# Window attention and convolution on one core: softmax weights as the stationary operand, a new order of the steps

## The reference

```python
x = x + _L0_conv_ref(_gn(x), L0_conv_ac_w, L0_conv_ac_b, L0_conv_qkv_w, L0_conv_proj_w, L0_conv_proj_b)
x = x + _L1_conv_ref(_gn(x), L1_conv_W, L1_conv_bias)
```

```python
g = (x * ac_w[None, :, None, None] + ac_b[None, :, None, None]) * x
g = jnp.clip(g, 0.0, 6.0)
qkv = jnp.einsum('bchw,dc->bdhw', g, qkv_w)
...
attn = jnp.einsum('wnqd,wnkd->wnqk', q, k) * scale
attn = jax.nn.softmax(attn, axis=-1)
o = jnp.einsum('wnqk,wnkd->wnqd', attn, v)
...
out = jnp.einsum('bchw,dc->bdhw', o, proj_w) + proj_b[None, :, None, None]
```

## Time and profile before

| | us |
|---|---|
| median of 3 runs | 1495.81 (1494.65 to 1499.69) |
| the profiled execution | 1495.76 |
| its span | 1494.0 |
| PE busy | 1171.3 (78%) |
| DVE busy | 1232.3 (82%) |
| ACT busy | 994.7 (67%) |
| POOL busy | 620.4 (42%) |

### The profile page before, as it was taken

How to read it: one execution, slowest core, us unless ns; L and a number is a source line. 1 busy time by engine, 2 the same in 40 slices (tenths; PEclk the granted TensorE clock), 3 DMA queues, 4 the chain that set the end, 5 groups by cost and what they waited for, 6 DMA issues and landing times. The chain is left out here.

```text
span 1494.0 us, 56299 instructions
## 1 busy us (share of the span) xinstructions
PE 1171.3 (78%) x21860; PEld 696.7 (47%) x21860; DVE 1232.3 (82%) x1891; ACT 994.7 (67%) x1683; POOL 620.4 (42%) x438
## 2 busy tenths in 40 slices
PE   1288888988898986878747888988898898768875
PEld 1155555655565654333324555555565565423332
DVE  6678778887887985999985878887887888679998
ACT  2768777877787874544425877877787788644442
POOL 7124333433334432565632333333333334336665
PEclk9989999999999997899987999999999999979999
DMA  6143333333333330032324333333333343101111
GB/s 249 55 124 105 114 106 95 123 107 94 114 115 93 124 106 4 29 112 84 112 98 147 111 116 98 109 113 102 104 115 104 104 125 113 30 0 57 42 56 70
DMA packets 115466, 144.93 MB, mean 97 GB/s; under 512 B 21000, under 2 KB 91048, under 8 KB 114216
## 3 DMA queue, kind: packets, MB, share of 16 engines
q1 hardware_dynamic: 115240, 141.44, 29.6%
HBM read 72.16 MB, written 69.24 MB: 95 GB/s over the span
## 5 line engine op out<-in xcount | busy, mean ns | idle before, releaser
L503 ACT ACTIVATE work<-ps,ws 128x512 f32<-128x512 f32 x512 | 337.1, 682 | 61.8 <-PE ps L972 42.8
L734 DVE TENSOR_REDUCE m_all<-ps 128x8 f32<-128x512 f32 x512 | 328.1, 683 | 45.2 <-PE ps L949 44.0
L409 POOL TENSOR_TENSOR work<-work 128x512 f32<-128x512 f32 x128 | 162.7, 1271 | 370.4 <-ACT work L511 370.4
L415 POOL TENSOR_TENSOR g_lo<-work,g_hi 128x512 f16<-128x512 f32 x128 | 145.6, 1158 | 327.9 <-ACT g_hi L548 327.9
L960 PE MATMUL ps<-q_stack,k_stack 128*64 128x64 f16 x8192 | 216.4, 200 | 25.7 <-DMA q_stack<-max_scratch 24.0
L960 PEld LDWEIGHTS ps<-q_stack,k_stack 128*64 128x64 f16 x8192 | 179.4, 114 | 84.3 <-DMA q_stack<-max_scratch 45.4
L972 PE MATMUL ps<-work,v_ext 128*32 128x64 f32 x8192 | 210.1, 226 | 6.5 <-ACT work L503 0.6
L906 PE MATMUL ps<-work,c_hi 128*128 128x512 f16 x384 | 150.5, 392 | 69.6 <-DVE work L825 69.5
L601 ACT CAST work<-work 128x640 f16<-128x640 f32 x128 | 92.0, 720 | 145.6 <-DVE work L821 99.6
L949 PE MATMUL ps<-k_stack,q_stack 128*64 128x256 f16 x2048 | 177.8, 291 | 13.8 <-issue 4.8
L972 PEld LDWEIGHTS ps<-work,v_ext 128*32 128x32 f32 x8192 | 137.2, 110 | 92.0 <-issue 69.3
(11 more groups left out here) (130 smaller groups left out, 2022.9 us busy)
## 6 DMA issues: line engine op xcount, KB each, us to landing
stack_scratch<-work SPq DMA_DIRECT2D x128, 256.0 KB, 2.1
q_stack<-stack_scratch SPq DMA_DIRECT2D x64, 384.0 KB
k_stack<-stack_scratch SPq DMA_DIRECT2D x256, 96.0 KB
stack_scratch<-work SPq DMA_DIRECT2D x128, 128.0 KB, 2.1
out_dram<-work SPq DMA_DIRECT2D x32, 512.0 KB, 2.7
img<-in_x_dram SPq DMA_DIRECT2D x8, 1024.0 KB, 14.2
img<-in_x_dram SPq DMA_DIRECT2D x16, 512.0 KB, 3.9
q_stack<-zero_scratch SPq DMA_DIRECT2D x64, 32.0 KB
```

Source lines behind the costliest of these rows:

```text
L409: g.tensor_tensor(recip[h], sums[h], guess[h], ALU.mult).then_inc(near_done, 1)
L415: g.tensor_tensor(g_lo[:, m, :, e, :], g32.rearrange("p (w q) -> p w q", w=UW), g_hi[:, m, :, e, :], ALU.subtract).then_inc(g_lo_done, 1)
L503: a.activation(probs[:, w % 2, :], ps[:, ST_B + w % 2, :], ACT.Exp, scale=ws[:, R_EXP:R_EXP + 1]).then_inc(exp_done, 1)
L734: v.tensor_reduce(m_all[:, 0, 2 * h:2 * h + 2, p, :], ps[:, S_B + h, :].rearrange("p (g j k) -> p g j k", g=2, k=WIN), AX.X, ALU.max).then ...
```

## The change

- `weigh` swaps the operands: the exponentials (64 columns, f32) are stationary, `v_ext` (now 18 columns: 16 for two heads, 2 for row sums) moves. The result has queries in the rows and, for each of 8 head pairs, 18 columns. Two windows (a pair `p`) are one step of 16 products; there were two steps of 8.
- `divide` takes the exact reciprocal of the sums (128 x 32) and multiplies 256 columns with it. Shuffle, guesses and Newton step are gone.
- `turn` transposes the result back (two f32 transposes for each half of a unit), ACT copies it (`turned`), and `output` is one product with the whole projection matrix.
- `scores_t`, `exps`, `scores` and `row_max` work on two PSUM banks at a time: four steps a unit each, 1024 columns a step on ACT and DVE.
- The first product of scores uses 96 rows, not 128; the zeros that were loaded for it (L307) go.
- v is computed in one step into bank GB, with the two heads of a pair in two halves of the rows. Half of `g_hi` and `g_lo` (a second copy of each) goes.
- The second pass of unit n starts in iteration n at its windows 0 to 3 and ends in iteration n+1 (stage E); the maxima are sent in D; R is two iterations behind.

```diff
-                return {s for s, lead in (("G", 4), ("H", 3), ("B", 2), ("C", 1), ("D", 0), ("R", -1), ("X", -2))
+                return {s for s, lead in (("G", 4), ("H", 3), ("B", 2), ("C", 1), ("D", 0), ("E", -1), ("R", -2))
...
-                        v.stream_shuffle(sums[h], ps[:, PV_B + h, :], [16 + j % 16 for j in range(32)]).then_inc(sums_done, 1)
...
+                        bank = ps[:, PV_B + h, 0:2 * HP * VC].rearrange("p (a c) -> p a c", c=VC)
+                        after(dve, pv_done, d, 2 * h + 2)
+                        v.reciprocal(rec[h], bank[:, :, 2 * HD:VC]).then_inc(rec_done, 1)
...
-                            v.tensor_reduce(m_all[:, 0, 2 * h:2 * h + 2, p, :],
-                                            ps[:, S_B + h, :].rearrange("p (g j k) -> p g j k", g=2, k=WIN), AX.X,
-                                            ALU.max).then_inc(max_done, 1)
+                        v.tensor_reduce(m_all[:, 0, :, p, :],
+                                        ps[:, S_B:S_B + 2, :].rearrange("p h (g j k) -> p (h g) j k", g=2, k=WIN), AX.X,
+                                        ALU.max).then_inc(max_done, 1)
...
+                        a.activation(probs[:, p % 2, :], ps[:, ST_B:ST_B + 2, :].rearrange("p w t -> p (w t)"), ACT.Exp,
...
+                                mm = t_.matmul(ps[64 * w:64 * w + 64, PV_B + p // 2, col:col + VC],
+                                               probs[:, p % 2, at:at + WIN], v_ext[:, md, 2 * p + w, hp, :],
                                                start=True, stop=True)
...
-                            mm = t_.matmul(ps[:, GB, :], pw[:, a, :], o_n[:, :, a, :], start=(a == 0), stop=(a == 1))
+                        t_.matmul(ps[:, GB, :], pw[:, :], o_t, start=True, stop=True).then_inc(proj_done, 1)
...
+                    if "C" in on:
+                        scores(1)
+                    if "E" in on:
+                        weigh(n - 1, me, 2)
                     if "B" in on:
+                        after(pe, v_out, n + 1)
                         after(pe, res_done, n - 2)
                         project(1, GB, k_done)
+                    if "E" in on:
+                        scores_t(n - 1, me, 3)
```

More of the change, by code:

```diff
@@ L308, in one @@
+                        write(d, mb, 1)
                         after(sp, q_sent, d)
+                        after(sp, st_done, d - BUFS)
                         sp.dma_start(q_stack[0:ROWS, mb, :, :],
@@ new lines, in v_rows @@
+                    def v_rows():
+                        r_hi, r_lo = (r[:, 2, :].rearrange("p (h e d) -> p e h d", e=2, d=HD) for r in (w_hi, w_lo))
+                        for w in range(UW):
+                            tok = slice(w * WIN, (w + 1) * WIN)
+                            l_hi, l_lo = g_hi[:, mb, tok], g_lo[:, mb, tok]
+                            for k, (lhs, rhs) in enumerate(((l_hi, r_hi), (l_lo, r_hi), (l_hi, r_lo))):
+                                for e in range(2):
+                                    mm = t_.matmul(ps[64 * e:64 * e + 64, GB, tok], lhs, rhs[:, e, :, :],
+                                                   start=(k == 0), stop=(k == 2))
@@ L977, in output @@
[L977 to L989 removed]
+                                                   q_stack[0:ROWS, mc, 2 * h + gg, tok],
@@ new lines, in scores, with scores_t @@
+                                                   k_stack[0:ROWS, mc, 2 * h + gg, :, tok], start=True, stop=True)
+                        mm.then_inc(s_done, 1)
+                    def scores_t(d, md, p):
+                        after(pe, exp_done, d, p)
+                        for w in range(2):
+                            tok = slice((2 * p + w) * WIN, (2 * p + w + 1) * WIN)
+                            for hp in range(HP):
+                                g, j = hp // 2, 2 * (hp % 2)
+                                for e in range(2):
+                                    mm = t_.matmul(ps[64 * e:64 * e + 64, ST_B + w, hp * WIN:(hp + 1) * WIN],
+                                                   k_stack[:, md, g, j + e, tok], q_stack[:, md, g, tok],
+                                                   start=True, stop=True)
+                        mm.then_inc(st_done, 1)
@@ new lines, in turn @@
+                    def turn(d, h):
+                        after(pe, o_done, d, h + 1)
+                        for a in range(2):
+                            mm = t_.transpose(ps[:, GA, h * 256 + a * P:h * 256 + a * P + P], o_n[h][:, a * P:a * P + P],
+                                              ident[:, :])
+                        mm.then_inc(ot_done, 1)
+                    def output(d):
+                        after(pe, ot_out, d)
+                        t_.matmul(ps[:, GB, :], pw[:, :], o_t, start=True, stop=True).then_inc(proj_done, 1)
```

444 lines of the change are left out of this document (181 added, 263 removed).

## The result

The changed kernel takes 1672.62 us (median, 1664.65 to 1678.25), where the kernel before took 1495.23 us beside it (1493.36 to 1499.69): a ratio of 1.118 [1.113, 1.123]. It is slower, as forecast, but by 177 us, not 59, and the time lies above the range of 1470 to 1615 us. The span of the profiled execution is 1676.5 us, 182.5 more than before.

What follows compares the result with a forecast made beforehand. The keys' loop through DRAM was taken to bound the kernel: 7.7 + 8.3 = 16.0 us a unit instead of 14.74. That gave +29.7 us per image, +59 for two on 1495.76: 1555 us, range 1470 to 1615.

Steps and rivals of the forecast that it cites:

- The second loop: Keys leave DVE, go through DRAM and back to the next unit's scores; 13.9 of 14.74 us, close to the bound.
- The 0.8 us of slack: Room left in the keys' loop of the kernel before: 5.1 + 8.8 = 13.9 of 14.74 us a unit.
- that of the maxima: Maxima written to DRAM and read back: a little later, but used later too, at 9.1 us, so hidden.
- X: Time from a unit's first scores until DVE finishes the keys: 7.7 us, 2.6 more than before.
- L: Time from finished keys through DRAM to their use in the next unit's scores: 8.3 us.
- P: Length of an ordinary attention unit, X + L: 16.0 us instead of 14.74.
- `weigh`'s 1.03: On PE, a `weigh` step of 32 pairs, priced by its f32 loads: 1.03 us, bounds 0.58 and 1.43.
- The clock in ordinary units: PE's clock was taken as low only behind the loop's branch, one unit in three; ordinary units take 16.0 us.
- rival 3: PE's clock falls in ordinary units too, up to +1.6 us each: 1590 to 1600 us if in all; chance 0.18.
- the unit behind the branch: It starts at 1.2 GHz, which makes scores, the first `weigh` and part of a projection longer: 17.6 us.
- The loop's end: PE's pause of 3.6 to 4.0 us at the branch is partly covered by the wait for keys: unit of 17.3 us.
- The tail: Second pass and new stage at an image's end: guesses, POOL products and half an `output` go, transposes and copies come: -3 us.

Runs made afterwards that it cites:

- old_keys: The changed kernel, but the first scores use q and k of the unit before, so no new keys are waited for: 1502.85 us.
- keys_first: The changed kernel with the keys' projection right behind that of q on PE, their copies moved up on ACT and DVE: 1544.15 us, 1.032 of before.
- before_late: The kernel before with only PE's projection of k moved behind the second step of scores: 1654.06 us, 1.107 of before.
- warm: The changed kernel with 30 unread f16 products on PE ahead of the first scores in each full unit: 1624.9 us, 1.088 of before.
- after_vc32: The changed kernel with 32 moving columns in `weigh` in place of 18, the added ones zeros: 1637.14 us, 1.093 of before.
- keysfirst_vc32: `keys_first` with 32 moving columns in `weigh` in place of 18, the added ones zeros: 1501.92 us, 1.004 of before.
- warm2: As `warm`, but without the 30 unread products in the unit right behind the loop's branch: 1615.62 us, 1.084 of before.

## Why the prediction was right and wrong

- **The bound.** Right. The second loop, not DVE, was what the change ran into: taking the wait for keys out (`old_keys`) or most of it (`keys_first`) gives back 180 and 127 us of the 182.5 in the span. The 0.8 us of slack read from the earlier trace rows was the reading that mattered. In the kernel before there was a second such loop beside it, that of the maxima, which the prediction called hidden; in the changed one it is, but `before_late` shows that it was near.
- **X = 7.7, L = 8.3, P = 16.0.** X was 7.7 us in eight of the ten units (of 59) whose part up to the low half of k ran at full clock (7.9 and 8.2 in the others). Right were also `weigh`'s 1.03, the exponential's 1.12 and the order on DVE. L was 7.3 to 8.3 in the eight units at full clock (mean 7.7) and 8.46 over the 59, so that P at full clock was 15.5 on average, not 16.0: L was taken 0.6 us too long for them. The reciprocal of 128 x 32 was priced at 0.2 and takes 0.36 us:

```profile
361.65 0.36 DVE L657 RECIPROCAL work<-ps 128x32 f32<-128x32 f32 x1 [0.26 <-PE ps L904]
```

  It didn't matter, as DVE is at 60%, not near the 70% that I named.
- **The clock in ordinary units: the step that failed.** The forecast had PE at 2.4 GHz in them, and rival 3, with a chance of 0.18, had it fall. It fell: in 9 of the 14 ordinary units of the loops and in all 14 with the branch. `old_keys` and `warm` show that the wait for keys does it in the ordinary ones: with no wait, or with work in its place, none of the 14 has any time at 1.2 GHz. Measured over 59 units X was 9.85 us, where the steps give 8.08 (7.7, and 9.3 in the 14 units behind a branch): 1.77 x 59 = 104 us of the 123 us by which the span was missed. The tails below are most of the rest.
- **The size of rival 3 and of the unit behind the branch.** Both were priced with a stretch of 3.4 us at the low clock, +1.6. The price for a microsecond was right (0.48 measured); the length was wrong: 6.3 us a unit on average, 8.3 on average behind the branch, where it was 2.9 before. I took it from the earlier trace rows, a stretch of the kernel before in which PE, once it worked again, had other work; the added columns (`after_vc32`, `keysfirst_vc32`) show that the form of `weigh` is part of the difference. Rival 3's sum was also too small by its own price: 1.6 us in all 32 units that neither have the branch nor stand behind it is 51 us, 1606, and with the 14 that have the branch 1629, not 1590 to 1600. Both are why 1672 lies above it.
- **The loop's end.** 17.3 was forecast for a unit with the branch. With a warm clock it is (`warm2`, 17.0 to 18.0); in the changed kernel it takes about 20, again by its clock (0.77).
- **The tail, -3 us per image: wrong.** From an image's last first scores to the start of POOL's last add it takes 50.7 and 42.8 us in the two images, where it took 35.4 and 34.3. These 24 us are most of the other 28; the first two units of the second image are 3 more. The windows of both tails of the changed kernel:

```profile
646.33:697.07 50.74, 44.68 (x725) 34.77 (x725) 11.68 (x20) 16.15 (x22) 3.82 (x4) 0.50 0.02 5
1449.36:1492.15 42.79, 35.29 (x725) 26.81 (x725) 11.57 (x20) 16.08 (x22) 3.82 (x3) 0.70 0.02 5
```

  the same stretches of the kernel before, and the first tail of `after_vc32`, which has the same instructions and 14 columns of zeros more to each product of `weigh`:

```profile
555.66:591.03 35.37, 24.20 (x564) 15.35 (x557) 21.58 (x34) 19.45 (x32) 10.89 (x10) 0.81 0.02 5
1276.99:1311.27 34.28, 23.08 (x563) 14.47 (x557) 21.01 (x34) 19.37 (x32) 10.87 (x10) 0.85 0.02 5
...
634.90:669.76 34.86, 26.69 (x725) 20.29 (x725) 11.75 (x21) 15.97 (x22) 3.81 (x4) 0.96 0.03 7
```

  At a clock of 0.96 the new tail is as long as the old one was at 0.81 and 0.85. So the 24 us are the low clock again, which the tail's sum left out; only the missing gain of 3 us an image is left, which may be the chain of exponential, `weigh` and `scores_t` that I hadn't followed; that isn't shown.

What is shown and what isn't: that the wait for keys is most of the loss is shown by `old_keys`, which keeps every instruction and changes only what the first scores read and where PE waits. That this wait pulls the clock down in ordinary units is shown by `old_keys` and `warm`. That `weigh`'s few moving columns help to hold it down is shown by adding idle ones, twice. What keeps the changed kernel's clock at 0.869 even then is in the table: it falls as often as before the edit. `after_vc32` and `warm` were not run in one kernel. And it isn't shown why the clock stays low longer behind the branch even in `old_keys` (8.8 us) than in the kernel before (2.9); the form of `weigh` is a candidate, as 14 added columns take it from 8.2 to 5.2 us in `keys_first`.

## What to carry to other kernels

Before a step is moved on an engine, follow what it makes through DRAM and back to its next use, and add up the loop; here 2.6 us later on one engine lengthened every unit, while three engines got lighter for nothing; and look which engine's queue stands behind the copy of what was moved. Where the weight loads set PE's pace and the moving operand is narrow, pad it as far as it costs nothing and look at the clock's row: here that was worth 2 to 3%. And a turn of a hardware loop with more in it is the cheapest gain of this study: 32 us on the old kernel with an edit of four lines. A wait of one engine also costs what its clock does afterwards, so price both.

## What the runs showed of the hardware

- Adding 14 columns of zeros to each product of `weigh` raised the granted clock from 0.828 to 0.869, and from 0.863 to 0.915, at no cost of its own.
- The clock can stay low for a whole unit while PE is never idle: 21.47 us busy of 21.47, behind a wait of 1.03 us; the same work at full clock takes 13.6. In the changed kernel it fell 47 times in the two attention phases, and 15 and 14 times, about once a branch, with the wait for keys taken out or filled.
- Two kernels whose units at full clock have busy shares that look alike, 13.47 of 17.00 us and 12.91 of 16.02, had mean clocks of 0.922 and 0.828.
- Filler products right behind the loop's branch run at 1.2 GHz themselves: the 30 of `warm` take 4.96 us there and 2.64 elsewhere.
- With a 384 KB read issued some 0.65 us ahead of a write, the write could be used 4.5 us after its issue in the median of the units, against 2.2 us with the read behind it.
- A branch of the hardware loop stops PE for 3.3 to 4 us in the changed kernel and, with the low clock that follows, cost 4.0 us of the kernel's time in the old order and 5.4 in the new.
